# Attention with layer norm, 16 images: fp32 score tiles of 64x32 on two key halves, block transposes and four PV tiles in place of fp32r scores and TensorE transposes

## What is computed

```python
q, k, v = proj(wq, bq), proj(wk, bk), proj(wv, bv)      # (B, 8, S, 64)
scores = einsum('bhqd,bhkd->bhqk', q, k) / sqrt(64)
scores = scores + spatial_bias[:, 0][dist]              # dist = |dh| + |dw| of two tokens
attn = softmax(scores, axis=-1)
ctx = einsum('bhqk,bhkd->bhqd', attn, v)                # back to (B, S, 512)
resid = ctx @ wo + bo + x
out = layernorm(resid) * ln_gamma + ln_beta
```

## Time and profile before

| what | value |
|---|---|
| time, three runs | 4176.31 us median (4156.1 to 4186.96) |
| profiled execution, its span | 4168.2 us |
| TensorE busy (matmul) | 3974.2 us, 95% of the span |
| VectorE busy | 2776.1 us, 67% |
| ScalarE busy | 2443.8 us, 59% |
| GpSimd busy | 644.4 us, 15% |

### The profile page before, as it was taken

How to read it: one execution, slowest core, us unless ns; L and a number is a source line. 1 busy time by engine, 2 the same in 40 slices (tenths; PEclk the granted TensorE clock), 3 DMA queues, 4 the chain that set the end, 5 groups by cost and what they waited for, 6 DMA issues and landing times.

```text
span 4168.2 us, 74488 instructions
## 1 busy us (share of the span) xinstructions
PE 3974.2 (95%) x26624; PEld 3254.2 (78%) x26624; DVE 2776.1 (67%) x5393; ACT 2443.8 (59%) x4742; POOL 644.4 (15%) x648
## 2 busy tenths in 40 slices
PE   3999999999999999999999999999999999999998
PEld 3888878788787877878778787787877878788786
DVE  3676757667576775767767676675766757667676
ACT  2674746647466474655746557465674756747464
POOL 0003012030110302103021030200203012030113
PEclk8999999999999999999999999999999999999999
DMA  5121211212121121212211122111221111211111
GB/s 141 39 61 47 57 43 56 62 51 60 44 57 53 55 57 54 56 43 65 59 47 55 39 69 56 49 51 45 63 62 48 54 45 56 62 51 56 47 53 46
DMA packets 119844, 230.45 MB, mean 55 GB/s; under 512 B 15336, under 2 KB 57320, under 8 KB 119416
## 3 DMA queue, kind: packets, MB, share of 16 engines
q1 hardware_dynamic: 99657, 157.40, 14.3%
q10 hardware_dynamic: 19760, 67.51, 5.0%
HBM read 131.65 MB, written 33.92 MB: 40 GB/s over the span
## 4 chain that ended last, share of the span: by engine, by line
PE 82%; ACT 7%; DMA 5%; issue 3%; DVE 3%; SPq 1%; POOL 0%; DVEq 0%; POOLq 0%; ACTq 0%
PE pv_ps L629 18%; PE s_ps L592 16%; PE t_ps L606 16%; PE spare_ps L542 9%; PE pv_ps L542 5%; PE spare_ps L569 4%; PE pv_ps L555 4%; PE spare_ps L555 4%; PE pv_ps L569 4%; ACT prob L709 3%; ACT prob_t L727 2%; DMA wqk_sb<-wqk_split 2%; DMA tokens<-in_x 1%; ACT q_sb L699 1%; DMA bias_by_w<-bias_grid 1%
## 5 line engine op out<-in xcount | busy, mean ns | idle before, releaser
L727 ACT ACTIVATE prob_t<-t_ps 120x480 f32<-120x480 f32 x1920 | 993.2, 571 | 799.2 <-PE t_ps L606 798.4
L592 PE MATMUL s_ps<-k_sb,q_sb 128*120 128x450 f32 (+2 forms) x4096 | 1031.0, 376 | 84.2 <-DVE q_sb L832 45.0
L709 ACT ACTIVATE prob<-prob,row_min 120x900 f32<-120x900 f32 (+1 forms) x960 | 1009.5, 1052 | 39.4 <-DVE row_min L853 33.1
L853 DVE CUSTOM_DVE_ANT_0 prob<-s_ps,window 120x900 f32<-120x900 f32 x896 | 975.6, 1089 | 35.0 <-PE s_ps L592 29.5
L606 PE MATMUL t_ps<-ident,prob 120*120 120x120 f32 x7680 | 962.2, 268 | 10.5 <-DVE prob L866 10.1
L606 PEld LDWEIGHTS t_ps<-ident,prob 120*120 120x120 f32 x7680 | 830.2, 137 | 176.5 <-issue 56.9
L629 PE MATMUL pv_ps<-prob_t,values 120*64 120x240 f32 x8192 | 853.5, 362 | 26.5 <-ACT prob_t L727 20.8
L592 PEld LDWEIGHTS s_ps<-k_sb,q_sb 128*120 128x120 f32 (+2 forms) x4096 | 705.5, 180 | 188.6 <-issue 80.5
L629 PEld LDWEIGHTS pv_ps<-prob_t,values 120*64 120x64 f32 x8192 | 594.6, 140 | 268.7 <-issue 85.3
L866 DVE TENSOR_SCALAR prob<-prob,row_inv 120x900 f32<-120x900 f32 (+1 forms) x960 | 765.8, 798 | 33.8
L542 PE MATMUL spare_ps<-xt,wqk_sb 128*128 128x450 f32 x2112 | 524.2, 380 | 0.0
(11 more groups left out here) (73 smaller groups left out, 2934.3 us busy)
## 6 DMA issues: line engine op xcount, KB each, us to landing
wqk_sb<-wqk_split ACTq DMA_DIRECT2D x126, 512.0 KB, 3.8
k_sb<-k_sb SPq DMA_DIRECT2D x252, 225.0 KB, 3.4
tokens<-in_x SPq DMA_DIRECT2D x212, 240.0 KB, 3.0
out<-tokens SPq DMA_DIRECT2D x105, 240.0 KB, 2.4
tokens<-in_x SPq DMA_DIRECT2D x30, 120.0 KB, 3.2
wqk_split<-k_sb SPq DMA_DIRECT2D x8, 256.0 KB, 3.7
wqk_split<-ctx_t SPq DMA_DIRECT2D x8, 256.0 KB, 3.9
out<-tokens SPq DMA_DIRECT2D x15, 120.0 KB, 1.9
```

Of the source, the lines that this page charges most:

```text
L592: last = pe.matmul(s_ps[0:n, u % 2, half, 0:HALF], q_sb[:, p % 2, head, q0:q0 + n], k_sb[:, p % 2, head, part, half * HALF:half * HALF + H ...
L709: nc.scalar.activation(prob[0:n, u % BUFS, 0:S], prob[0:n, u % BUFS, 0:S], ACT.Exp, scale=-1.0, bias=row_min[0:n, s:s + 1], accum_out=row_ ...
L727: nc.scalar.activation(dst, src, ACT.Copy).then_inc(moved, 1)
L853: nc.vector.tensor_tensor_reduce(halves(prob[0:n, u % BUFS, 0:S]), s_ps[0:n, u % 2, :, 0:HALF], halves(bias.rearrange("p a c -> p (a c)")) ...
```

## The change

A unit becomes 60 queries (two grid rows) of both heads against all keys. The scores of a unit lie in PSUM on partition blocks of 32: block 2a + r holds grid row a (30 of its 32 rows are queries) against key half r (450 keys), one bank per head.

- `scores`: queries and keys are plain fp32, no longer split. Eight matmuls per unit, each 64 rows by 32 columns by 450. They are issued for two units at a time, 6 units ahead (`AHEAD = 6`, was 3).
- Softmax goes in two halves: each partition block has the minimum and the sum of its own key half. `exchange` (SP) sends both to the neighbouring block by four small DMAs per two units, `leads` and `totals` (GpSimd), `ratios` (ScalarE) and `weights` (VectorE reciprocal) make one factor per row, head and unit out of them.
- `normalise` moves from VectorE to ScalarE: `activation(..., Copy, scale=weight)`, two of 450 columns per unit, after two `exponentials` of 450.
- `turn` (VectorE): one transpose in 32x32 blocks of 128x960 per unit takes the place of TensorE's transposes and of ScalarE's moves of them.
- `context`: 15 key blocks of 32, for each four matmuls (two grid rows by two heads) of 64 rows, 64 columns, 120 moving columns (90 in the last group of a pair); `keep_context` moves the result to `ctx_sb` in fp32.
- The values are laid out by key block: `stage_value` and `keep_value` write them to DRAM, `load_values` reads them back in the new order, by pair. The bias of v goes through wo once, in the prologue.
- `split_context` (GpSimd) makes the hi and lo halves of the context, just ahead of `out_tile`. The hi and lo halves of q, k, and `copy_keys` are gone. `keep_piece` is one ScalarE operation of 128x450.
- The background work is placed by `place` by a number of steps per two units (2 where there is a PV group, else 8); four token slots in place of two.

The core of the diff:

```diff
-ROWS = 4
-TT = ROWS * GRID
+TT = 120
+QUAD = 32
+BLOCKS = -(-HALF // QUAD)
+SK = BLOCKS * QUAD
-PER_PAIR = NT * 2 - 1
+PER_PAIR = GRID // 2
-AHEAD = 3
-EXP_AHEAD = 2
-NORM_AHEAD = 1
-BUFS = 4
+AHEAD = 6
+RING = 6
+STATS = 3
+SLOTS = 4
+PV_UNITS = [4, 8, 12, 16, 20, 24, 28, 30, 34, 38, 42, 46, 50, 54, 58, 60]
+XT_UNITS = [30, 30, 32, 32, 34, 34, 36, 36]
+SPLIT_UNITS = [0, 0, 4, 7, 8, 11, 14, 16]
+PV_STEPS, FULL_STEPS = 2, 8
...
-                for half in range(2):
-                    for head, q0, n in blocks:
-                        for part in range(2):
-                            last = pe.matmul(s_ps[0:n, u % 2, half, 0:HALF],
-                                             q_sb[:, p % 2, head, q0:q0 + n],
-                                             k_sb[:, p % 2, head, part, half * HALF:half * HALF + HALF],
+                if not known(unit, 1):
+                    pe.wait_ge(scores_min, 2 * (unit - 1))
+                for a in range(2):
+                    q0 = GRID * (2 * v + a)
+                    for r in range(2):
+                        row = 2 * QUAD * a + QUAD * r
+                        for head in range(2):
+                            d = slice(DK * head, DK * head + DK)
+                            last = pe.matmul(s_ps[row:row + QUAD, u % 2, head, 0:HALF], q_sb[d, p % 2, q0:q0 + QUAD],
+                                             k_sb[d, p % 2, columns(r)], start=True, stop=True, skip_group_check=True)
...
-                for k in range(NT):
-                    for head in range(2):
-                        f = (2 * p + head) * DK
-                        last = pe.matmul(pv_ps[DK * head:DK * head + DK, 0:n], values[0:TT, k, f:f + DK],
-                                         prob_t[:, head, k, 0:n], start=(k == 0), stop=(k == NT - 1),
+                for j in range(BLOCKS):
+                    for a in range(2):
+                        half = slice(2 * QUAD * a, 2 * QUAD * a + 2 * QUAD)
+                        for head in range(2):
+                            d = slice(DK * head, DK * head + DK)
+                            last = pe.matmul(pv_ps[d, a, 0:n * GRID].rearrange("d (u w) -> d u w", u=n),
+                                             values[half, p % 2, j, d],
+                                             prob_t[half, g % 2, 0:n, head, QUAD * j:QUAD * j + GRID],
+                                             start=(j == 0), stop=(j == BLOCKS - 1), skip_group_check=True)
...
+            def body(im, u):          # TensorE
+                if u % 2 == 0:
+                    for x in (u + AHEAD, u + AHEAD + 1):
+                        if im.live(x):
+                            scores(im, x)
+                g = group_at(u)
+                if g is not None:
+                    context(im, g)
+                for work in im.background(u):
+                    work_on(im, work[:-2], *work[-2:])
...
+            def body(im, u):          # ScalarE
+                if im.live(u + AHEAD):
+                    exponentials(im, u + AHEAD)
+                if u % 2 and im.live(u + 3):
+                    ratios(im, u + 3)
+                if im.live(u + 2):
+                    normalise(im, u + 2)
...
+            def normalise(im, u):     # ScalarE
+                act.wait_ge(weight_done, im.b * (UNITS // 2) + u // 2 + 1)
+                for head in range(2):
+                    nc.scalar.activation(prob[:, u % RING, head, 0:HALF], prob[:, u % RING, head, 0:HALF], ACT.Copy,
+                                         scale=weight[:, s, c:c + 1]).then_inc(prob_done, 1)
...
+            def body(im, u):          # VectorE
+                if im.live(u):
+                    turn(im, u)
+                if u % 2 == 0 and im.live(u + 2):
+                    weights(im, u + 2)
+                if im.live(u + AHEAD):
+                    biased_scores(im, u + AHEAD)
...
+            def turn(im, u):          # VectorE
+                dve.wait_ge(prob_done, 2 * im.unit(u) + 2)
+                nc.vector.transpose(out=prob_t[:, g % 2, v % PER_GROUP, :, :].rearrange("p h k -> p (h k)"),
+                                    in_=prob[:, u % RING, :, :].rearrange("p h k -> p (h k)")).then_inc(turned, 1)
...
+            def leads(im, x):         # GpSimd
+                pool.wait_ge(exchanged[s], 64 * (im.b * (UNITS // 2 // STATS) + x // 2 // STATS + 1))
+                nc.gpsimd.tensor_tensor(lead[:, s, :], own[:, s, 0, :], other[:, s, 0, :], ALU.subtract)
+                nc.gpsimd.tensor_scalar(lead[:, s, :], lead[:, s, :], CLAMP, None, ALU.min)
...
+            def totals(im, x):        # GpSimd
+                nc.gpsimd.tensor_tensor(total[:, s, :], ratio[:, s, :], other[:, s, 1, :], ALU.mult)
+                nc.gpsimd.tensor_tensor(total[:, s, :], total[:, s, :], own[:, s, 1, :], ALU.add)
...
+            def body(im, u):          # GpSimd
+                if u % 2 == 0 and im.live(u + 2):
+                    totals(im, u + 2)
+                if u % 2 and im.live(u + 3):
+                    leads(im, u + 3)
+                for work in im.out_tiles(u - 2):
+                    scale_shift(im, work)
+                for work in im.out_tiles(u - 1):
+                    reciprocal_std(im, work)
+                for work in im.out_tiles(u + 1):
+                    add_bias(im, work)
+                for t in range(NT):
+                    if SPLIT_UNITS[t] == u and not im.first:
+                        split_context(im, ("out", t))
...
+            def exchange(im, x):      # SP
+                sp.wait_ge(exp_done, 2 * im.unit(x + 2))
+                for a in range(4):
+                    c = a ^ 1
+                    sp.dma_start(other[QUAD * a:QUAD * a + QUAD, s, :, :], own[QUAD * c:QUAD * c + QUAD, s, :, :]
+                                 ).then_inc(exchanged[s], 16)
```

More of the change, by code:

```diff
@@ L130 @@
[L130 to L150, removed]
@@ L153, in works_of @@
[L153 to L169, removed]
+KEY, QUERY = 0, 1
@@ new lines, in bank_of, with wanted @@
+def bank_of(item):
+    if item[0] in ("first_xt", "final"):
+        return item[1] % 2
+    if item[0] == "bv_wo":
+        return 0
+    return BANK[item]
+def wanted(item, first, last):
+    if item[0] == "out":
+        return not first
+    if item[0] in ("xt", "value") or item[0] == "piece" and item[1] >= PAIRS:
+        return not last
+    return True
+def background(u, first, last):
+    work = [("xt", t, 0, KT) for t in range(NT) if XT_UNITS[t] == u and not last]
+    work += [(*item, k0, k1) for item, k0, k1 in STEPS.get(u, []) if wanted(item, first, last)]
+    if last:
+        work += [("final", t, 0, KT) for t in range(NT) if FINAL_UNITS[t] == u]
+    return work
@@ new lines, in order, with evicted, out_tiles @@
+def order(first, last):
+    return [w[:-2] for u in range(END) for w in background(u, first, last) if w[-1] == KT]
+def evicted(u, first, last):
+    items = [("xt", t) for t in range(NT) if XT_UNITS[t] + 1 == u and not last]
+    items += [item for item in SEQUENCE if EVICT.get(item) == u and wanted(item, first, last)]
+    if last:
+        items += [("final", t) for t in range(NT) if FINAL_UNITS[t] + 1 == u]
+    return items
+def out_tiles(u, first, last):
+    return [w for w in evicted(u, first, last) if w[0] in ("out", "final")]
@@ L177, in __init__, with start, use, pair @@
         self.b, self.first, self.last = b, first, last
-    def start(self, bank, what):
-        before, in_first, in_middle = COUNTS[bank][what]
+        self.units = END if last else UNITS
+        self.order = order(first, last)
+    def start(self, bank):
+        before, in_first, in_middle = COUNTS[bank]
         return before + (0 if self.first else (self.b - 1) * in_middle + in_first)
[L184 to L199, removed]
+    def use(self, item):
+        bank = bank_of(item)
+        return self.start(bank) + in_bank(self.order, bank).index(item)
     def unit(self, u):
         return self.b * UNITS + u
+    def pair(self, p):
+        return self.b * PAIRS + p
+    def group(self, g):
+        return self.b * GROUPS + g
+    def live(self, u):
+        return not (self.first and u < 0) and not (self.last and u >= UNITS)
+    def background(self, u):
+        return background(u, self.first, self.last)
+    def evicted(self, u):
+        return evicted(u, self.first, self.last) if u >= 0 else []
+    def out_tiles(self, u):
+        return out_tiles(u, self.first, self.last) if u >= 0 else []
 class Prologue:
@@ L664, in _ @@
             images(pe, body)
-            end = Image(B - 1, last=True)
-            context(end, GROUPS - 1, end.uses_before_unit(UNITS, 1))
-            for work in background(UNITS, False, True):
-                out_tile(end, UNITS, work)
         @block.scalar
@@ L740, in _ @@
-            pro = Prologue()
+                use = ("piece", p, j)
+                bank, pair = bank_of(use), im.pair(p)
+                if not known(pair, 1):
```

(5 more changed lines are left out.)

1088 lines of the change are left out of this document (552 added, 536 removed).

## The result

The changed kernel takes 4242.39 us (4235.55 to 4250.4, 4 runs) against 4171.57 us before (4156.1 to 4186.96, 4 runs): a ratio of 1.0164, 95% interval 1.0127 to 1.0202. It is slower by 1.6%, where the prediction said 3,570 us.

What follows compares the result with a forecast made beforehand. The prediction took TensorE's summed work to bound the old kernel. After the change, TensorE 190 us plus 28 for handovers gave 218 per image; 16 images plus 75 came to 3,563, rounded to 3,570 us; range 3,230 to 4,180.

Steps and rivals of the forecast that it cites:

- What bounds the kernel before, and the pace of its matmuls: Kernel before the change: bound by TensorE's summed work, 240 of 256 us per image, with 16 us of waits and handovers.
- TensorE after: TensorE's work in the changed kernel: 190 us per image with all tiles running at once, key transposes gone.
- Rival 1: TensorE: only two matmul passes run at once, making its work 365 us per image and the kernel 5,950 us; chance 0.14.
- rival 3: TensorE: scores run four at a time or weight loads serially, adding 45 to 55 us per image; 4,100 to 4,250; chance 0.06.
- Dispatch: TensorE's sequencer: at most 35 ns per load and matmul, which would put its upper end at 212 us per image.
- Rival 2: TensorE's instruction dispatch binds: 50 ns per matmul gives 239 us per image, an 83 ns floor 5,675 us total; chance 0.05.
- ScalarE and VectorE: Work of these two engines in the changed kernel: 189 us (bounds 178 to 200) and 175 us per image.
- GpSimd and DMA: GpSimd about 90 us per image, its late sums costing 8; exchange of maxima, landing in 3.4 us, just hidden.
- The sum: Whole kernel: TensorE's 190 us plus 28 for handovers gives 218 per image; 16 images plus 75 us give about 3,570.
- Rival 4: Handovers bind, not an engine: exchange or GpSimd late by about 1.5 us per two units; 240 us per image, 3,930; chance 0.12.
- The clock: TensorE's granted clock: read as 2.4 GHz nearly throughout before the change, and passes afterwards priced at 2.4 GHz.
- What was named as proof: Signs in the trace: scores unit 0.75 to 0.9 us, PV 3.0 to 3.7, ACT near 85% busy; otherwise multiplication waiting for sums.

Runs made afterwards that it cites:

- e8: Changed kernel with the multiplication by the weights moved back from ScalarE to VectorE, behind the biased scores: 4431.11 us, ratio 1.0648.
- e3: Changed kernel without exchange, leads, ratios and totals, each key half dividing by its own sum: 3982.94 us, ratio 0.9558.
- e13: Changed kernel with VectorE's reciprocal of the sums behind the biased scores of its step instead of ahead: 4096.33 us, ratio 0.9845.
- e1: Changed kernel with ScalarE emptying background banks right behind a unit's exponentials, ahead of ratios and multiplication: 4049.04 us, ratio 0.9717.
- e10: Changed kernel with background spread evenly, 5 and 5 steps instead of 2 and 8, which also makes evictions nearer: 3941.31 us, ratio 0.9476.
- e4: Changed kernel with PV multiplying only 8 of the 15 key blocks: 4247.8 us, ratio 1.0188.
- e14: e12 with ScalarE's ratios ahead of the unit's exponentials instead of behind the evictions: 3817.43 us, ratio 0.9163.
- e12: Changed kernel with early bank eviction on ScalarE, background spread 5 and 5, and the late reciprocal on VectorE together: 3696.3 us, ratio 0.8896.
- e6: Changed kernel plus 16 unused filler matmuls where TensorE waits for a bank, six times per image: 4202.28 us, ratio 1.0088.

## Why the prediction was wrong

- **What bounds the kernel before, and the pace of its matmuls: right.** Nothing in the runs speaks against it.
- **TensorE after: right, to 1%.** 192 us of work for a forecast 190. The tiles do run at once: scores 0.835 us a unit (forecast 0.83), PV 3.24 (forecast 3.0, upper end 4.2). Rival 1 (two passes at once, scores 3.0 us) and rival 3 (1.5 us) fall. That the sum is so close is in part luck: PV is 49 for 45 and the rest 93 for 88, and the 7 us for changes of tile shape, forecast apart, are inside the measured distances. The "80 of start" stood in no row; it is the 0.16 us at the end of each two units. Two slips in the working are harmless: the short PV group is 2.66 in the earlier trace rows and not 2.6, and 64 columns at 0.86 ns are 55 ns and not 53.
- **Dispatch: right.** 120 loads and matmuls in 3.24 us are 27 ns each, below the 35 read from the earlier trace rows. Four passes at a time, 102.5 ns apart, are already 26 ns each, so the passes set this pace and not the dispatch. Rival 2 falls. The Trainium skill, "TensorE: Matmul & The Clock Gate", "Back-to-back issue gap", has 25 ns or about 62. The trace rules out the second for this kernel and does not measure the first.
- **ScalarE and VectorE: right in size.** Busy 174 and 162 us per image for 189 and 175. The forecast had about 10 us of DMA issues in ScalarE's sum and 6 of waits in VectorE's, which busy time does not count. e8 shows that the multiplication belongs on ScalarE rather than on VectorE.
- **GpSimd and DMA: 74 us for 90.** The exchange lands in 1.7 us (median of 1,920), the forecast took 3.4. It was called "just hidden", and GpSimd's late sums 8 us per image; taking the merge out gives 16 (e3), and letting the biased scores not queue behind it gives 9 (e13).
- **The step that failed is "The sum":** "Today the longest alone loses 16 us; here I add 28". The term for handovers was 28 us, and measured it is 260 less 192, 68 us per image: 47 of TensorE's waits and some 18 by the clock. The 40 us more in 16 images are 640 of the 672 us of the miss, and the 2 us more of TensorE's work the other 32. The 28 was a guess by analogy with the kernel before, whose one full engine hid everybody's waits; no view was read for it, and the clock was not in it. The lists of the change itself could have been: 8 steps hold parts of three items on two banks, and the third needs a ScalarE eviction that stands behind exponentials, ratio and multiplication of a unit (2030.40 to 2032.92 above). That such waits bind is shown by e1, e10 and e13, which only move instructions; how the 68 us divide among the moves is not, since their gains overlap.
- **Rival 4** (3,930 us, chance 0.12) had the mechanism, handovers and not an engine, but its place (exchange and GpSimd) is only one of several. Each alone on the changed kernel: places with nearer evictions 301 us, the whole merge out 259 (e3), eviction order 193, late reciprocal 146. The rival added 22 us per image to the forecast where 40 were missing, and so did not reach the other side. Break-even was a handover term of about 63 us per image, with TensorE at 192.
- **The clock** was taken as full. That held for an engine 95% busy, and not here: 0.900. e4 shows it from the other side: less work, a clock of 0.879, and no time gained.
- **What was named as proof** worked in part: scores and PV pace came out as "right", "ACT near 85% busy" as wrong (66%). The predicted sign of rival 4, the multiplication waiting for the sums, was not what the trace shows: L807 hardly waits at all. The wait for the sums stands one engine earlier, on VectorE's reciprocal (L931, 23 times for 30 pairs of units, 31.9 us), and the exponentials wait for VectorE's minima (71.6 us).

## What to carry to other kernels

A change that takes work off the engine that binds can lose all of it again to waits, which that engine's load had covered, unless the lists are ordered for it. Before a price is put on "three engines near each other", read for each wait on a PSUM bank what stands ahead of its eviction in the other engine's list, and count how many items a stretch of work opens on how many banks. Here three such edits, which only move existing instructions, were worth 13% (4242 to 3696 us), more than the change itself moved; and a test that takes a piece of one engine's work out (e4) tells in one run whether that piece is the matter. Sum a view of waits over several periods: a window of one period can count a wait at its edge twice.

## What the runs showed of the hardware beside that

- fp32 matmuls on 64x32 tiles ran 7.2 passes at once of 8 possible, on 64x64 tiles 3.7 of 4, though each matmul is two passes on its own tile; between the ends they start in full groups of eight and four. On 64x64 tiles a pass of 120 columns takes 262 ns and one of 90 takes 237, which is 0.83 ns or 2 clocks per column, as in the earlier trace rows. I had given only two at once 14 chances in 100.
- A block transpose of 128x960 fp32 takes VectorE 1,174 ns, 1.22 ns per column.
- In the image shown, the work behind each gap of TensorE of 2.5 to 7.2 us ran at 1.2 GHz, at once or within 1 us; behind two gaps of 1.9 and 1.1 us close together it did so too, behind the other short ones it ran at 2.4. The run's mean clock went roughly with the busy share of TensorE on the page: 0.879 at 75% (e4), 0.900 at 80% (the changed kernel), 0.930 at 86% (e14), 0.955 at 87% (e12), 0.988 at 95% (the kernel before). Matmuls that do nothing, put into the gaps, paid for themselves (e6).
- A DMA of 1 KB from one block of partitions to its neighbour lands in 1.7 us, while the timeline of the changed kernel shows its queue held 0.59 us for the issue.
